# First batch in a new order on all engines, and the last batch's reciprocals spread by TensorE, in a fused attention and spiking feed-forward layer

## The reference, cut to what matters

```python
xn = _layernorm(x, axis=-1)
Q, K, V = (split_heads(xn @ W.T + b) for W, b in ((Wq, bq), (Wk, bk), (Wv, bv)))
Q, K = _rope(Q, pos), _rope(K, pos)
scores = where(causal, einsum('bhqd,bhkd->bhqk', Q, K) * scale, NEG_INF)
attn = einsum('bhqk,bhkd->bhqd', softmax(scores), V)
h = square(relu(einsum('bsd,fd->bsf', xn, W_fc)))
y = einsum('bsf,df->bsd', h, W_proj)
for _ in range(5):
    reset = spike_fn(mem - 1)
    mem = 0.9 * mem + y - reset
    spks += spike_fn(mem - 1)
out = x + (concat(attn) @ Wo.T + bo) + spks / 5
```

## Time and profile before

| what | value |
|---|---|
| median of 3 runs | 2170.7 us (2169.31 to 2172.22) |
| profiled execution, its own time | 2166.99 us |
| its span | 2165.3 us |
| TensorE busy | 2088.6 us, 96% |
| ScalarE, VectorE, POOL busy | 67%, 64%, 51% |
| first scores start | 69.29 us |
| last numerator copied, last sum begins | 2134.87 us, 2158.37 us |

### The profile page before, as it was taken

The page is one execution under the profiler, slowest core; times in us unless marked ns, Lnnn a source line. Parts: engine busy times, 40 slices in busy tenths (PEclk is TensorE's granted clock), DMA queues, the critical chain, the costliest instruction groups (busy, mean ns, idle before and its releaser), DMA issues.

```text
span 2165.3 us, 67675 instructions
## 1 busy us (share of the span) xinstructions
PE 2088.6 (96%) x25492; PEld 1510.5 (70%) x25492; DVE 1385.3 (64%) x2139; ACT 1444.7 (67%) x1676; POOL 1111.0 (51%) x1072
## 2 busy tenths in 40 slices
PE   5999999999999999999999999999999999999995
PEld 4677676777767677676777767677676777767663
DVE  7576585766758566585666758566585666757443
ACT  3666667676676767667667676767667667676662
POOL 5464463645546455464645546455463645646341
PEclk9999999999999999999999999999999999999998
DMA  5353636445364553635445364553635445364442
GB/s 200 120 165 95 186 103 170 128 120 184 93 178 119 138 168 95 193 106 158 140 120 180 93 179 120 135 172 95 195 106 155 143 120 178 91 175 126 113 115 71
DMA packets 169866, 299.97 MB, mean 139 GB/s; under 512 B 25104, under 2 KB 114960, under 8 KB 157200
## 3 DMA queue, kind: packets, MB, share of 16 engines
q1 hardware_dynamic: 169616, 296.10, 47.6%
HBM read 174.89 MB, written 103.28 MB: 128 GB/s over the span
## 4 chain that ended last, share of the span: by engine, by line
PE 81%; ACT 4%; DMA 4%; DVE 4%; issue 3%; SPq 2%; POOL 1%; ACTq 0%; DVEq 0%; POOLq 0%
PE pair L1530 22%; PE pair L1327 21%; PE pair L1513 12%; PE pair L1336 9%; PE pair L1305 7%; PE pair L1253 5%; PE pair L1319 4%; ACT probs L813 3%; SPq L441 2%; DMA recip_rows<-recip_dram 2%; DMA qk_dram<-rot_b 1%; PE pair L1271 1%; PE pair L1468 1%; DVE xn L951 1%; DVE rot_b L1004 0%
## 5 line engine op out<-in xcount | busy, mean ns | idle before, releaser
L813 ACT ACTIVATE probs<-pair 128x1024 f32<-128x1024 f32 x1152 | 1139.7, 1029 | 503.8 <-PE pair L1513 502.0
L688 POOL TENSOR_TENSOR h_lo<-h_sq,h_hi 128x512 fp32r<-128x512 f32 x256 | 409.9, 1601 | 478.0 <-DVE h_hi L1072 477.6
L1336 PE MATMUL pair<-wproj_hi,h_hi 64*128 64x256 f32 x2048 | 590.1, 288 | 0.0
L1336 PE MATMUL pair<-wproj_hi,h_lo 64*128 64x256 f32 x2048 | 572.3, 279 | 0.0
L1336 PE MATMUL pair<-wproj_lo,h_hi 64*128 64x256 f32 x2048 | 571.6, 279 | 0.0
L1327 PE MATMUL pair<-xT_hi,wfc_hi 64*128 64x256 f32 x2048 | 551.0, 288 | 6.4 <-DVE fin L1019 2.5
L696 POOL TENSOR_SCALAR_AFFINE_SELECT probs<-probs 128x512 f32<-128x512 f32 x512 | 376.4, 753 | 341.9 <-ACT probs L813 341.9
L1530 PE MATMUL pair<-probs,v_sb 128*17 128x512 f32 (+3 forms) x6144 | 545.3, 488 | 0.9 <-ACT probs L813 0.9
L1327 PE MATMUL pair<-xT_lo,wfc_hi 64*128 64x256 f32 x2048 | 536.0, 280 | 0.0
L1327 PE MATMUL pair<-xT_hi,wfc_lo 64*128 64x256 f32 x2048 | 535.2, 279 | 0.0
L1513 PE MATMUL pair<-q_ring,k_ring 64*128 64x512 f32 (+3 forms) x3072 | 442.4, 355 | 19.6 <-ACT probs L813 14.1
(11 more groups left out here) (113 smaller groups left out, 2901.8 us busy)
## 6 DMA issues: line engine op xcount, KB each, us to landing
q_ring<-qk_dram SPq DMA_DIRECT2D x384, 128.0 KB
k_ring<-qk_dram SPq DMA_DIRECT2D x384, 128.0 KB
qk_dram<-planes SPq DMA_DIRECT2D x64, 512.0 KB, 2.8
qk_dram<-rot_b SPq DMA_DIRECT2D x62, 512.0 KB, 3.8
xn<-in_x SPq DMA_DIRECT2D x16, 1024.0 KB, 5.6
rs<-in_x SPq DMA_DIRECT2D x64, 256.0 KB, 2.8
acc_dram<-rs SPq DMA_DIRECT2D x64, 256.0 KB, 2.2
attn<-numer SPq DMA_DIRECT2D x256, 64.0 KB, 2.4
```

Source lines behind the costliest of these rows:

```text
L688: pool.tensor_tensor(h_lo[i % HB][:, :], h_sq[i % HB][:, :], h_hi[i % HB][:, :].bitcast(F32), ALU.subtract).then_inc(h_lo_done, 1)
L813: act.activation(probs[BUFFER[n]][:, 2 * pr:2 * pr + 2, :], pair[m % NSLOT][:, :, :], ACT.Exp, scale=SCALE).then_inc(exp_done, 1)
L1336: return pe.matmul(proj_bank[:, t * D:(t + 1) * D], h[rows, a * T2 + t * P:a * T2 + (t + 1) * P], w[rows, f, :], start=i % ITEMS_OF_GROUP ...
```

## The change

**Opening.** TensorE makes 24 transposes of the identity first, then its own. Then the first four items are expanded in two pairs of turns before any is contracted (four PSUM banks instead of two); `opening` has 12 turns instead of 14. In interval 0 the contractions of the last four items (before: two) run beside the four values. ScalarE loads the square root's table before anything else and the exponential's at the end of the opening; it takes over square and rounding of items 0 to 2. The square root of batch 1 comes from ScalarE and VectorE instead of POOL. VectorE takes one half of the low part of wfc and the fourth sum. The high planes have four buffers and the squares a place of their own, so that x of batch 1 is loaded right behind the transposes; each plane is stored as soon as it is there. The ring's 13 transfers are issued by SP (five) and ScalarE (eight). add_bias of batch 0 and what follows it on VectorE and SP move to steps 2 and 3 of interval 0. Table and constants:

```diff
+FIRST_TURNS, ON_SCALAR = 12, 3
+WARM_UP, NORMS_BEHIND, BIAS_BEHIND = 24, 5, 7
+VALUES_FIRST = {(0, 0): (0, 0), (0, 1): (0, 1), (0, 3): (1, 0), (0, 4): (1, 1), (1, 0): (2, 0), (1, 1): (2, 1),
+        (1, 3): (3, 0), (1, 4): (3, 1)}
+TAKE_V_FIRST = {(0, 3): (0,), (1, 0): (1,), (1, 3): (2,), (1, 4): (3,)}
+Y_CARRIED_FIRST, BARE_AT = (1, 4), (2, 4)
...
-first_fc_bank = halves[0]
-first_norm_bank, bias_bank = pair[1][:, 0, :], pair[1][:, 1, 0:D]
+first_fc_bank = halves[0] + halves[1]
+first_norm_bank, bias_bank = fc_bank[0], fc_bank[1][:, 0:D]
+first_squares = over("first_squares", [P, 4, 2, G], BF16, probs_at + 16 * KB)
...
+first_planes = planes + [over(f"first_planes{i}", [P, 2, G], F32R, probs_at + (8 + 4 * i) * KB) for i in range(2)]
...
+FIRST_PARTS_Q, FIRST_PARTS_K = ((0, 0), (1, 0)), ((0, 0), (1, 1), (2, 0))
+def first_ring(eng, dst, is_k, part, lo):
+    for eo in range(2):
+        eng.dma_start(dst[2 * part + eo:P:NF, 0, :, :].bitcast(F32),
+                      qk_dram[0, is_k, lo, eo].rearrange("(r t) s -> r t s", t=NTILE)[:, 0:2, :]
+                      ).then_inc(ring_in[0], 16)
```

SP, opening; then POOL, opening:

```diff
     def opening():
-        for u in range(4):
-            store_planes(0, 0, u, first_rot_b)
-        load_x(0, 1)
+        alone(sp, xT_ps, 4)
+        sp.dma_start(xn[:, :, :], rows(x, 1)).then_inc(x_in, 16)
+        for u, lo in ((0, 0), (0, 1), (1, 0), (1, 1), (2, 0), (2, 1), (3, 0), (3, 1)):
+            first_store(u, lo)
+        for u in range(2):
+            alone(sp, first_out[u], 2 * 16)
+            sp.sem_inc(planes_out[u], 2 * 16)
         alone(sp, shift_used, 1)
         store_shift(0, shift_out)
         for s in planes_out:
             alone(sp, s, 4 * 16)
+        sp.wait_ge(cleared, 4)
+        for part, lo in FIRST_PARTS_Q:
+            first_ring(sp, q_ring, 0, part, lo)
         alone(sp, shift_out, NG * 16)
-        sp.wait_ge(cleared, 4)
-        load_ring(-1, 0, 0, None)
+        sp.dma_start(q_ring[6:P:64, 0, :, :].bitcast(F32), shift_dram[0, :, 0:2, :]).then_inc(ring_in[0], 16)
         load_rs(0, 0, 0, False, False, half=1)
-        for a in range(2):
-            store_acc(0, 0, 0, a, False, half=1)
...
     def opening():
-        low_fc()
+        low_fc(0)
         low_proj(0)
+        sum_qk(0, 0, first_rot, first_rot_b)
+        sum_qk(0, 1, first_rot, first_rot_b)
         low_proj(1)
-        sum_qk(0, 0, first_rot, first_rot_b)
+        sum_qk(0, 2, first_rot, first_rot_b)
         low_proj(2)
-        sum_qk(0, 1, first_rot, first_rot_b)
+        h_low(0, 0)
         low_proj(3)
-        sum_qk(0, 2, first_rot, first_rot_b)
-        sum_qk(0, 3, first_rot, first_rot_b)
-        for i in range(NFT):
+        for i in range(1, NFT):
             h_low(0, i)
-        root(1)
-        pool.wait_ge(bias_done, 1)
-        for a in range(2):
-            add_bias(0, 0, a, False)
```

ScalarE:

```diff
+    def first_square(u):
+        act.wait_ge(rot_sum, u + 1)
+        act.activation(first_squares[:, u, :, :], first_rot[u][:, :, :], ACT.Square).then_inc(sq_done, 1)
+    def first_hidden(i):
+        sq, hi = h_sq[i % HB][:, :], h_hi[i % HB][:, :]
+        act.wait_ge(relu_done, i + 1)
+        act.activation(sq, sq, ACT.Square).then_inc(sq_h, 1)
+        act.wait_ge(sq_h, i + 1)
+        act.activation(hi, sq, ACT.Copy).then_inc(h_hi_done, 1)
+    def load_table(function):
+        act.activation(scratch[:, :], neg_half[:, :] if function == ACT.Exp else ln_b[:, :], function)
...
     def opening():
+        act.wait_ge(warm, 2)
+        load_table(ACT.Sqrt)
+        root_of_variance(0)
         high_weight(0)
-        root_of_variance()
...
         for n in range(4):
             high_xT(0, n, first_xT_bank)
         high_weight(2)
         high_weight(3)
-        plane_qk(0, 0, first_rot)
-        square_qk(0, 0, 0, first_rot)
-        plane_qk(0, 1, first_rot)
-        square_qk(0, 1, 0, first_rot)
+        high_weight(1)
+        first_plane(0)
+        first_square(0)
+        first_plane(1)
+        first_square(1)
         first_rectify(0)
+        first_hidden(0)
+        first_plane(2)
+        first_square(2)
+        first_plane(3)
+        first_square(3)
         first_rectify(1)
-        plane_qk(0, 2, first_rot)
-        square_qk(0, 2, 0, first_rot)
-        plane_qk(0, 3, first_rot)
-        square_qk(0, 3, 0, first_rot)
-        high_weight(1)
-        for i in range(2, NFT):
-            first_rectify(i)
+        first_hidden(1)
+        first_rectify(2)
+        first_hidden(2)
+        first_rectify(3)
+        first_rectify(4)
+        for s in planes_out:
+            act.wait_ge(s, 4 * 16)
+        act.wait_ge(cleared, 4)
+        for part, lo in FIRST_PARTS_K:
+            first_ring(act, k_ring, 1, part, lo)
+        first_rectify(5)
+        first_ring(act, q_ring, 0, 2, 1)
+        root_of_variance(1)
+        first_rectify(6)
+        first_rectify(7)
+        load_table(ACT.Exp)
```

VectorE, opening:

```diff
     def opening():
         first_statistics()
         variance(0)
-        small_constants()
-        first_root()
+        first_root(0)
         for t in range(NT):
             normalise(0, t)
         low_weight(0)
         for n in range(4):
             low_xT(0, n, first_xT_bank)
+        small_constants()
+        low_fc(1)
+        dve.wait_ge(table_in, 16)
+        dve.wait_ge(consts_done, 2)
+        for u in range(4):
+            first_rotate(u, 0)
+            first_rotate(u, 1)
+            if u in (1, 2):
+                first_low(u - 1)
+        first_sum(3)
+        first_low(2)
...
-        activate_h(0, 2)
+        dve.wait_ge(h_hi_done, ON_SCALAR)
+        activate_h(0, 3)
         low_weight(1)
-        activate_h(0, 3)
         whole_bias()
+        for t in range(NT):
+            statistics(1, t)
+        variance(1)
         activate_h(0, 4)
+        first_root(1)
+        activate_h(0, 5)
         take_y(ITEMS_OF_GROUP, 0)
-        activate_h(0, 5)
-        for t in range(4):
-            statistics(1, t)
         activate_h(0, 6)
+        for t in range(0, 4):
+            normalise(1, t)
+        activate_h(0, 7)
         for t in range(4, NT):
-            statistics(1, t)
-        activate_h(0, 7)
-        variance(1)
-        for t in range(NT):
             normalise(1, t)
-        for a in range(2):
-            alone(dve, rs_biased, a + 1)
-            dve.sem_inc(acc_done, 1)
...
-            if att and at == Y_CARRIED_AT:
+            if first and at == BARE_AT:
+                for a in range(2):
+                    alone(dve, rs_biased, a + 1)
+                    dve.sem_inc(acc_done, 1)
+            if att and at == (Y_CARRIED_FIRST if first else Y_CARRIED_AT):
                 take_y(items_before(b, again), NTG - 1)
             if (more or final) and at in y_at:
```

TensorE, opening:

```diff
+    def await_first(i, turn):
+        if turn:
+            pe.wait_ge(fc_turn, i + 1)
+        elif i < HB:
+            pe.wait_ge(rot_done, 2 + i // 2)
+        else:
+            pe.wait_ge(relu_done, i - HB + 1)
     def first_turn(t):
         k, turn = t // 2, t % 2
-        if k == 0:
-            expand_together(0, 0, 0, turn, False, opens=True)
+        i, j = (2 * k, None) if k < 2 else (k + 2, k - 2)
+        await_first(i, turn)
+        if j is None:
+            await_first(i + 1, turn)
         else:
-            expand_and_contract(0, 0, k + 1, k - 1, turn, None, 0 if k > 1 else None, False, opens=True)
+            if j < ITEMS_OF_GROUP and turn == 0:
+                pe.wait_ge(w_lo[3], j + 1)
+            await_contract(0, j, turn)
+        for n in range(PART):
+            h = expand_part(i, turn, n, first_fc_bank)
+            y = expand_part(i + 1, turn, n, first_fc_bank) if j is None else contract_part(j, turn, n)
+        h.then_inc(fc_ps if turn else fc_turn, 1)
+        if j is None:
+            y.then_inc(fc_ps if turn else fc_turn, 1)
+        else:
+            y.then_inc(proj_done if turn else proj_turn, 1)
...
     def opening():
+        for t in range(WARM_UP):
+            pe.transpose(first_xT_bank[3][:, t % 4 * P:(t % 4 + 1) * P], ident, ident)
...
-        norms(0, first_norm_bank)
-        pe.wait_ge(w_lo[3], 4)
-        for t in range(2, 6):
+        for t in range(FIRST_TURNS):
             first_turn(t)
-        pe.wait_ge(wo_in, 16)
-        pe.wait_ge(bias_rep, KD)
-        split_product(bias_bank, [(bv_rep[:, k, :], wo_sb[:, k, :]) for k in range(KD)]).then_inc(bias_ps, 1)
-        for t in range(6, 2 * NFT - 2):
-            first_turn(t)
+            if t == NORMS_BEHIND:
+                norms(0, first_norm_bank, first_squares)
+            if t == BIAS_BEHIND:
+                pe.wait_ge(wo_in, 16)
+                pe.wait_ge(bias_rep, KD)
+                split_product(bias_bank, [(bv_rep[:, k, :], wo_sb[:, k, :]) for k in range(KD)]
+                              ).then_inc(bias_ps, 1)
```

**Last batch.** `closing` takes the place of `last_output`. TensorE multiplies the half k=0 of attn by wo before the reciprocals exist, and spreads them over the partitions by products with a constant matrix of zeros and ones (`spread_sb`, loaded at step 13 of the last interval over `planes`). `fin` is loaded at step 16 of the last interval. SP, VectorE and TensorE:

```diff
+    def load_last_fin(b):
+        for n in range(4):
+            alone(sp, out_sent[n], b * 16)
+        for a in range(2):
```

(53 more changed lines are left out.)

170 lines of the change are left out of this document (104 added, 66 removed).

## The result

The changed kernel takes **2160.9 us** (median of 5 runs, 2158.0 to 2161.5) against 2170.7; the ratio is 0.995, 95% interval 0.9937 to 0.9963. It is faster, by 9.8 us and not by 24.6, and outside the range of 2140 to 2156. The profiled execution took 2157.99 us (span 2156.2) against 2166.99 (span 2165.3).

A forecast was written before the change was run, and what follows sets the result against it. The prediction took TensorE's own work to bound the loop (busy 128.90 of 130 us), so only the ends could gain: tail 13.4 plus opening 11.2 is 24.6, 2170.7 - 24.6 = 2146.1 us; range 2140 to 2156.

The forecast's parts named there:

- the tail: Last batch: no DRAM trip for reciprocals, half the output product done ahead; last sum ends at 2145.6 against 2159.06, 13.4 us saved.
- rival (2): Last batch: its last products run at half clock or numer_in lands late, 3.5 us more, 2149.6 us; chance 0.08.
- the first contraction: Opening: TensorE's first contraction waits for h_low(0) on POOL until 37.9 us, or 34.5 or 35.8 without port cost.
- The warm-up: Opening: 24 transposes ahead of the real ones bring nothing, as the clock is full, and take back 0.7 us.
- landing 2.3 later, 54.5: Opening: ScalarE's last ring issue ends at 52.2 us, its transfer lands 2.3 later, so scores start at 54.5, not 69.29.
- two queues help: Opening's ring: DMA engines were only 0.32 busy, so issue is the limit; the second queue counted for 3 to 4 us.
- moves behind the ring ... and free[s] it: Opening: store_acc and load_rs on SP are issued behind the ring for quad 1, which frees the ring.
- granted clock 1.00 all through the opening; no idle stretch over 3 us: Opening, expected sign: TensorE keeps full clock throughout and has no idle stretch over 3 us before the scores.
- it counts in full: Whole kernel: a gain at the two ends counts in full, since the first batch's gain shifts every later batch forward.
- (1): Opening worth 3 to 8 us instead of 11, ring late or ScalarE's waits queue up; 2149 to 2154 us; chance 0.12.
- (3): Interval 0: a ScalarE and VectorE backlog gives back the opening's gain, only the 13.4 us stays; 2157.3 us; chance 0.05.
- (4): Opening: ScalarE's eight ring issues block it 4.99 us each, 34.0 us more, slower than before at 2180.1 us; chance 0.05.

The follow-up runs named there:

- a3: The kernel before with only the last batch's change, without the new opening: 2157.5 us, ratio 0.9933.
- a5: a2 with ten semaphore increments more at the start of POOL's program: 2155.1 us, ratio 0.9934 to the kernel before.
- a12: a2 with two semaphore increments more on POOL ahead of its opening's work: 2155.2 us, ratio 0.9907 to the kernel before.
- a7: a5 without the 24 warm-up transposes of the identity: 2151.0 us, ratio 0.9917 to the kernel before.
- a2: The changed kernel with SP waiting until the first ring slot's 13 transfers have landed before issuing the next loads: 2152.1 us, ratio 0.9915 to the kernel before.
- a8: a5 with POOL's low part of item 0 ahead of the third part of wproj: 2150.6 us, ratio 0.9912 to the kernel before.
- a11: a8 with all 13 transfers of the first ring issued by SP, none by ScalarE: 2154.2 us, ratio 0.9924 to the kernel before.
- a10: a8 without the 24 warm-up transposes of the identity: 2146.7 us, ratio 0.9889 to the kernel before.
- a6: The kernel before with 118 semaphore increments more at the start of POOL's program: 2178.1 us, ratio 1.0033.
- a13: a10 without its ten semaphore increments on POOL: 2155.2 us, ratio 0.9908 to the kernel before.

## Why the prediction was wrong

**Right: the tail.** 13.2 us in the profiled pair and 13.5 alone (a3), against 13.4. Each term held: two halves of 3.7 (3.4 and 3.5 in the sum), spread 2.0 (1.8), the fourth copy of the numerator as next late, full clock. The clock is not always full: in a5 and a12, two of the twelve profiles with the new tail, half clock fell into it, and from the numerator to the last sum it took 12.0 and 11.9 us instead of 10.2 to 10.3. That is rival (2), at half of its 3.5 us.

**Right, but partly by luck: the first contraction.** 37.88 against 37.9. The sum put the cost of working beside VectorE, 1.0 us, on POOL's low part of wfc, which took 2.41 as in the sum without it, and the first plane was ready 1.0 earlier than forecast (25.9, not 26.9). The cost then came elsewhere on POOL: on a low part of wproj (2.28 us, 1.28 alone), on the third sum (3.32) and on h_low(0) (2.25, 1.27 alone). The warm-up took back nothing (15.17 with and without it, a7) where 0.7 was said.

**Wrong: "landing 2.3 later, 54.5", and "two queues help".** The scores came 5.0 later. Term by term: ScalarE's issues started at 47.26 instead of 45.6, because the clock was at half behind the first contraction (45.6 to 45.8 in a2, a8 and a11, without a dip there); six took 5.38 instead of 4.44 (0.90 each, not 0.74). Together with the ReLU between them the last issue ended at 53.93 instead of 52.2, 1.7 late. The landing took 5.6 instead of 2.3, 3.3 more. The step that failed is the reading of a DMA share of 0.32 as room for a second queue ("so issue is the limit and two queues help"). It was an average that began before the ring did. While one queue issued the rest of the ring the share was 0.60, with two queues and nothing behind them 1.00 to 1.07 (a8), and with the next loads right behind 1.08. So the transfers set the time, and a landing of 2.3 us behind the last issue, the figure of one transfer in the earlier trace rows, was too short. Counted from the ring's first issue the scores were forecast after 8.9 us; they came after 12.3, of which 10.0 to 10.4 is the ring and about 2 the loads behind it. With the 1.7 us by which the first issue was late, that is the whole of the 5.0. The sentence that load_rs "moves behind the ring ... and free[s] it" got the direction wrong: what is issued behind the last ring transfer doesn't run behind it. a2 gives back 2 us of landing, a11 shows 0.6 for the second queue.

**Wrong: "granted clock 1.00 all through the opening; no idle stretch over 3 us".** The sum itself had the contraction waiting from 34.7 to 37.9, 3.2 us. I noted that wait and didn't charge for the clock behind it, though the earlier trace rows show the same pattern in before. In a8 the one long wait and the dip are gone, and the transposes of batch 1 come 3.1 us earlier than in a5. The dip isn't certain, though: a2 had none behind the same wait, and a10 had one behind a wait of 2.15 us.

**Wrong: "it counts in full".** The opening's 4.8 us arrived at batch 1; the tail's 13.2 at the end; between them 6.0 went to a stop that no line of the diff touches. I took unchanged code for unchanged time. a6 shows that even counting instructions on POOL bring the stop into the old kernel, and a13 against a10 that ten of them take it out. The +2.7 of the fourteen intervals can't be told from scatter: that stretch is 1822.1 to 1830.7 us in the twelve profiles with the new opening and 1823.3 to 1827.5 in the three with the old one, all with the same code in it.

**The rivals.** The time is that of none. (1) had its mechanism, a late ring, and named 3 to 8 us for the opening; it was 4.8. But it was put at 2149 to 2154, since the stop was in no case. (2) came in two profiles only, above. (3) named the right outcome for the wrong reason. (4) is out: 0.90 us an issue, not 4.99. a10, with the ring first, the low part ahead and no stop, has a median 25.1 us below before on its chip. That this meets the 24.6 of the sum is luck: the profiled executions of the two differ by 21.3 us in span, with `bound_max` of batch 1 earlier by 8.6, not 11.2, the tail shorter by 13.2, and 0.5 lost between them.

## What to carry to other kernels

A gain at the front of a long program has to be followed to the end: compare the two traces by marks in every stage, also where the code is the same. A share read off a stretch counts only if the stretch holds the work in question and nothing else. Before a second queue is counted as a gain, ask what will be in flight beside it, and hold the next loads until the urgent ones have landed; a low DMA share under one issuing queue isn't room that a second one gets. Each wait of TensorE that a plan accepts should be priced with the slow clock that can follow it, not with its length alone.
